# First layer of a four-layer float32 kernel: each expert product made of three float32r products, its input split on VectorE

## The reference, cut to what matters

```python
gate_probs = softmax(x @ gate_w.T + gate_b)            # [4096, 10]
weights, selected = top_k(gate_probs, 2)
# combine_w [4096, 8]: the two weights, null experts dropped, normalised
expert_out = einsum('td,edh->teh', x, expert_w) + expert_b
out = einsum('te,teh->th', combine_w, expert_out)      # summed over the 8 experts
```

## Time and profile before

| | |
|---|---|
| median of 3 runs | 1890.72 us (1885.95 to 1898.35) |
| profiled execution, time | 1888.65 us |
| profiled execution, span | 1886.9 us |
| PE / DVE / ACT / POOL busy | 1733.4 / 1019.3 / 830.8 / 377.3 us |
| granted PE clock, mean | 0.947 of full |
| L741 (expert product), 128 records | 72.8 us busy |

### The profile page before, as it was taken

One profiled execution on the slowest core, in us unless ns is written; L12 is line 12 of the kernel. 1 busy time (PEld: TensorE's weight loads), 2 busy tenths in 40 slices (PEclk: granted clock), 3 DMA queues, 4 the chain that ended last, 5 costly groups with the idle time before them and its releaser, 6 DMA issues. The chain is left out here.

```text
span 1886.9 us, 22763 instructions
## 1 busy us (share of the span) xinstructions
PE 1733.4 (92%) x8614; PEld 1012.4 (54%) x8614; DVE 1019.3 (54%) x1660; ACT 830.8 (44%) x1018; POOL 377.3 (20%) x306
## 2 busy tenths in 40 slices
PE   7599999998887998999999999999999987999996
PEld 4122222222544445787878787777878753444443
DVE  3444454553675444454544545455545546877785
ACT  4367777784533334333333433433433343334332
POOL 1000000000455001202030302021111105444442
PEclk8689999999876999999999999999999998999998
DMA  1232222221101750000000000000000010000001
GB/s 73 32 62 46 46 46 46 46 46 58 60 1 36 174 146 5 1 1 1 1 1 2 1 1 1 1 1 1 1 1 1 1 55 0 1 0 1 0 1 45
DMA packets 19128, 49.12 MB, mean 26 GB/s; under 512 B 784, under 2 KB 1680, under 8 KB 18128
## 3 DMA queue, kind: packets, MB, share of 16 engines
q1 hardware_dynamic: 19024, 47.70, 10.8%
HBM read 45.21 MB, written 2.36 MB: 25 GB/s over the span
## 5 line engine op out<-in xcount | busy, mean ns | idle before, releaser
L494 ACT ACTIVATE probs<-ps_ring 128x1024 f32<-128x1024 f32 x256 | 246.1, 1023 | 126.8 <-PE ps_ring L708 123.9
L1765 PEld LDWEIGHTS ps_o<-v,probs 128*128 128x128 f32 x2048 | 235.3, 192 | 31.0 <-issue 25.6
L1765 PE MATMUL ps_o<-v,probs 128*128 128x129 f32 x2048 | 248.1, 278 | 1.7 <-ACT probs L1490 1.2
L1490 ACT ACTIVATE probs<-ps_ring 128x1024 f32<-128x1024 f32 x128 | 127.0, 1024 | 212.0 <-PE ps_ring L1746 212.0
L722 PE MATMUL ps_o<-probs,v 128*32 128x512 f32 x1024 | 141.8, 628 | 13.1 <-DVE o_sb L545 13.1
L1571 DVE TENSOR_REDUCE negmax<-ps_o 128x2 f32<-128x1024 f32 x64 | 78.5, 1226 | 137.1 <-PE ps_o L1721 137.1
L1483 ACT ACTIVATE xn<-ps_ring,pack 128x512 f32<-128x512 f32 x64 | 40.6, 685 | 162.7 <-PE ps_ring L1330 162.7
L1944 POOL TENSOR_TENSOR rs<-r,state 128x512 f32<-128x512 f32 x64 | 81.9, 1280 | 150.2 <-DVE state L2091 150.2
L1584 DVE RECIPROCAL rden<-ps_o 128x2 f32<-128x2 f32 x128 | 21.5, 168 | 144.0 <-PE ps_o L1765 144.0
L708 PEld LDWEIGHTS ps_ring<-q_stack,k_stack 32*128 32x128 f32 x512 | 31.9, 188 | 125.0 <-issue 104.6
L2091 DVE TENSOR_TENSOR_SCAN state<-decay,state,kv 128x511 f32<-128x511 f32 x64 | 91.6, 1431 | 6.5 <-issue 1.1
(11 more groups left out here) (371 smaller groups left out, 3501.9 us busy)
## 6 DMA issues: line engine op xcount, KB each, us to landing
cwb<-combine_by_expert SPq DMA_DIRECT2D x8, 2048.0 KB
score<-score_by_expert SPq DMA_DIRECT2D x7, 2048.0 KB, 13.7
pack<-pack_dram SPq DMA_DIRECT2D x1, 3840.0 KB, 14.9
pack<-pack_dram SPq DMA_DIRECT2D x1, 2507.0 KB, 8.5
x<-x_in SPq DMA_DIRECT2D x2, 1024.0 KB, 6.3
out<-x SPq DMA_DIRECT2D x1, 2048.0 KB, 6.3
score<-score_by_expert SPq DMA_DIRECT2D x1, 1536.0 KB, 13.6
pack<-pack_dram SPq DMA_DIRECT2D x1, 1451.0 KB, 6.1
```

Of the source, the lines that this page charges most:

```text
L494: nc.scalar.activation(probs[n % 3][:, 2 * half:2 * half + 2, :], ps, ACT.Exp, scale=float(HD0) ** -0.5).then_inc(read, 1)
L1490: nc.scalar.activation(probs[:, n % 2, m, :, :], ps, ACT.Exp).then_inc(read, 1)
L1765: last = nc.tensor.matmul(ps_o[:, i, k * (D + 1):(k + 1) * (D + 1)], probs[:, (b * PAIRS + p) % 2, m, j, queries], v[:, m, h, :], start=(m ...
```

## The change

Each expert product becomes three float32r products by `split_products`. The weights of all eight experts are split once into `expert_high` (rounded) and `expert_low` (the rest), by DVE, behind `route_probs` and ahead of `scale_qk(0)`. A weigh now multiplies into `xe` (two buffers), drains, casts into `xe_high`, drains, and subtracts into `xe_low` (three buffers each). The wait for `xe_used` stands behind the multiply.

```diff
-        xe = sb("xe", [P, 3, T])
+        xe, xe_high, xe_low = sb("xe", [P, 2, T]), sb("xe_high", [P, 3, T]), sb("xe_low", [P, 3, T])
+        wide = E0_TRUE * P
+        expert_high, expert_low = sb("expert0_high", [P, wide]), sb("expert0_low", [P, wide])
...
+                nc.vector.tensor_tensor(xe[:, n % 2, :], xn[:, at(b)], cwb[:, e, :], ALU.mult)
+                dve.drain()
                 if n >= 3:
                     dve.wait_ge(xe_used, n - 2)
-                nc.vector.tensor_tensor(xe[:, n % 3, :], xn[:, at(b)], cwb[:, e, :], ALU.mult).then_inc(xe_ready, 1)
+                nc.vector.tensor_copy(single(xe_high[:, n % 3, :]), xe[:, n % 2, :])
+                dve.drain()
+                nc.vector.tensor_tensor(single(xe_low[:, n % 3, :]), xe[:, n % 2, :], xe_high[:, n % 3, :], ALU.subtract).then_inc(xe_ready, 1)
...
             route_probs()
+            nc.vector.tensor_copy(single(expert_high[:, :]), w["expert0"])
+            dve.drain()
+            nc.vector.tensor_tensor(single(expert_low[:, :]), w["expert0"], expert_high[:, :], ALU.subtract).then_inc(expert_split, 1)
             scale_qk(0)
...
                 pe.wait_ge(xe_ready, n + 1)
-                nc.tensor.matmul(ps_y[:, :], w["expert0"][:, e * P:(e + 1) * P], xe[:, n % 3, :],
-                                 start=(e == 0), stop=False).then_inc(xe_used, 1)
+                if n == 0:
+                    pe.wait_ge(expert_split, 1)
+                of = slice(e * P, (e + 1) * P)
+                split_products(nc, ps_y[:, :], (expert_high[:, of], expert_low[:, of]), (xe_high[:, n % 3, :], xe_low[:, n % 3, :]),
+                               e == 0, False).then_inc(xe_used, 1)
```

More of the change, by code:

```diff
@@ L415, in layer0_mix @@
         xe_ready, xe_used = sem("xe_ready"), sem("xe_used")
+        expert_split = sem("expert0_split")
         y_done, x_added = sem("y_done"), sem("x_added")
```

## The result

The changed kernel takes 1927.13 us (median of 4 runs, 1925.32 to 1937.42) against 1890.31 before: a ratio of 1.0209, 95% interval 1.0183 to 1.0234. It is slower by 37 us, where the forecast of 1905 meant some 15, and 1927 lies above the range of 1890 to 1918. The profiled execution took 1927.16 us, its span is 1925.4.

The account below looks back on a forecast made before the run. ACT was taken to pace up to step 12's scores, PE behind that, with DVE's order close to the front at steps 14 and 15. 8.8 + 4.5 + 0 + 3 = 16.3 us on 1888.65 gave 1905, range 1890 to 1918.

Parts of the forecast that it names:

- Three products for one, 0.89 us: Each expert on PE: three products take 0.89 us against 1.06 for the float32 one, a gain of 0.17 us.
- The weigh, 1.88 us and 2.02 to readiness: On DVE: a weigh occupies 1.88 us instead of 0.61, and `xe` is ready after 2.02 instead of 0.74.
- The split of the weights hidden, `copy_o(b, 2)` with cover left: Weight split, 2.0 us, fits DVE's 7.99 us idle before `scale_qk(0)`; `copy_o(b, 2)` keeps 0.7 us of cover.
- Waits of 1.8 at expert 6 and 0.86 at `replicate(b + 1, 1)`: Steps 14 and 15: PE idles 1.8 us for weigh 6, then 0.86 for `take_rep(b + 1, 0)` queued behind weigh 7.
- A block 1.46 us late: Each of blocks 1 to 6 ends 1.46 us late through DVE's order, 8.8 us in all.
- Block 7: 0: Last block, no `replicate` behind its weighs: PE's 1.0 us gain offsets the wait at expert 6; 0, between -1.4 and +0.5.
- The clock: New PE waits bring more stretches at 1.2 GHz, 1.2 us each: 2.5 stretches, 3 us, between 0 and 11.
- The sign of being wrong: Forecast wrong if `copy_o(b, 2)` came late too (weigh above 2.1 us) or block lengths spread by several clock stretches.
- the clock follows: Rival, 0.17: one more 1.2 GHz stretch in each of blocks 1 to 6, two in block 0; 8 x 1.2 = 9.6, giving 1912.
- PE's gain survives: Rival, 0.08: weighing stays hidden behind PE's order, all 64 product gains count, 10.9 us, giving 1878.
- A dearer weigh: Rival, 0.11: with POOL or the weights' DMA in the way a DVE weigh takes 2.4 us, giving 1918.
- Layers 1 to 3 unchanged: Sign expected in the changed trace: layers 1 to 3 stay as before; no size given.

Follow-up runs that it names:

- the products alone: Against the kernel before: three products per expert, weigh one multiply writing the rounded part, low part of weighted x left out (a fixed tile instead); 1883.73 us, 0.9962.
- the full-array product: Changed kernel plus one useless float32 128x128 by 512 product in step 0 of each block, ahead of `replicate(b, 2)`; 1928.84 us, 1.0198 of the kernel before.
- the 2.3 us of delay: Changed kernel plus three useless DVE copies ahead of `route()` in block 0, all later work 2.3 us later; 1925.62 us, 1.0196 of the kernel before.

## Why the prediction was wrong

- *Three products for one, 0.89 us*: right to the hundredth (219.47 to 220.36).
- *The weigh, 1.88 us and 2.02 to readiness*: measured 1.86 and 2.00 (217.47 to 219.47).
- *The split of the weights hidden, `copy_o(b, 2)` with cover left*: right, `copy_o` waited 1.11 us.
- *Waits of 1.8 at expert 6 and 0.86 at `replicate(b + 1, 1)`*: 1.75 and 0.67. *A block 1.46 us late*: 1.55 to 1.58 (that a block at full clock came out near the 48.7 named, at 48.46, is luck in part: 47.23 was 0.35 too much); block 0's `replicate(1, 1)` due at 122.54, found at 122.26. *Block 7: 0*: 0.8, above its upper bound of 0.5. Of order 13.3 us were worked out, and some 14.6 came.
- *The clock, "I take 2.5 stretches, 3 us, between 0 and 11"*: this is the step that failed. It was some 20 us in the first layer. The price of a fall was taken from the earlier trace rows as 1.2 us; that was misread, as the second window ends 0.35 us late, and a short fall costs 1.56. But at 2.5 falls this is one more microsecond. What was missing is the length: the prediction knew only short falls, while block 0 of the kernel before held one of 10.2 us (98.53 to 108.77) behind a wait of 1.08. In the new places a fall could last 17 us and cost 6 to 7 us a block, in three blocks. The argument against it, "each is shorter than one that already leaves the clock alone at 276.56", didn't hold: waits of 1.75, 0.64 and 0.46 us were followed by a fall, and one of 0.67 was not; the wait's length alone says nothing of it. The sign of being wrong that the prediction names at its end, block lengths that spread by several clock stretches, is what came: 48.5 to 55.8 us.
- The rival *the clock follows* named the cause and was mis-sized the same way (1912); its 8 x 1.2 us would have had to be some 20. *PE's gain survives* is what the kernels without the late waits show: 1884 with the products alone, where 1878 was worked out. *A dearer weigh* came true only in part, where POOL did the subtract.
- "Layers 1 to 3 unchanged" holds for the work. The 4.5 us behind the first layer were in no term; 3.4 of them are the two falls in the last layer, which other kernels' traces have or lack whatever was changed in the first.

Shown: the loss needs the late weighs. With only these split three quarters of it are there (28 us by the ratio), with only these whole none. About two fifths of the loss is order, and filling the idle time ahead of expert 6 takes 14 to 17 us back. Not shown: why the remaining quarter comes only when the early experts are split too. In blocks 1 to 6 falls of 10 us and more appear in the change, in the kernels with the full-array product and with the 2.3 us of delay, and where POOL subtracts; the kernel with the same waits and float32 products has none. These are one profile each, so it isn't excluded that the form of the products, together with the waits, has a part in how long a fall is. Open: what makes one fall 3 us long and the next 17, and why one short wait is followed by a fall and another not.

## What to carry to other kernels

On an engine with idle time, cost an addition by the first waiter behind it in program order; 60 us more of DVE were free in one place, and 18 dearer weighs behind `copy_o(b, 2)` cost 28 us in another. Where a new wait falls on PE, price the clock with it, from the worst fall that a trace of the kernel shows anywhere and not from the usual one, and cut two windows that are to be compared at the same instruction. And when such an addition loses, move it before giving it up: the same operations, reordered and left out of block 0, went from 1.0209 to 0.9985.

## What was not expected of the hardware

Behind equal waits of 1.75 us the granted clock held in one block (219.47), and dropped to 1.2 GHz in another for 17 us of nearly unbroken PE work (321 to 338), in which PE ran scores, `replicate`, `times_v`, expert 7 and `expert_bias`. There the rise fell within `project`; in the kernel delayed by 2.3 us it came 1.6 us ahead of it. The Trainium skill, "TensorE: Matmul & The Clock Gate", in its closing table, advises against idle gaps of more than about 3 us between bursts of matmuls. The runs here go further: they show falls behind waits of 1.75 us and, with the order moved, of 0.64 and 0.46 us. Beside POOL's subtract 17 of 56 casts took longer than their 0.43 us, up to 1.36, and 12 of 56 multiplies longer than 0.68, up to 1.70.
